# Softmax denominators in five blocks of matmul instead of seven, with one of five key additions on VectorE

## The reference

```python
scores = jnp.einsum('bhqd,bhkd->bhqk', q, k) / math.sqrt(HEAD_DIM)
causal = jnp.tril(jnp.ones((seq_len, seq_len), dtype=bool))
scores = jnp.where(causal[None, None, :, :], scores, jnp.float32(-1e+20))
attn = jax.nn.softmax(scores, axis=-1)
out = jnp.einsum('bhqk,bhkd->bhqd', attn, v)
```

## Time and profile before

| what | value |
|---|---|
| median of 3 runs | 1067.73 us (1065.66 to 1068.37) |
| the profiled execution's own time | 1066.51 us |
| its span | 1064.5 us |
| PE busy | 1017.9 us, 96% |
| PEld busy | 829.7 us, 78% |
| DVE busy | 636.3 us, 60% |
| POOL busy | 411.5 us, 39% |
| ACT busy | 399.5 us, 38% |
| mean granted TensorE clock | 0.983 |

### The profile page before, as it was taken

The page is one execution under the profiler, slowest core; times in us unless marked ns, Lnnn a source line. Parts: engine busy times, 40 slices in busy tenths (PEclk is TensorE's granted clock), DMA queues, the critical chain, the costliest instruction groups (busy, mean ns, idle before and its releaser), DMA issues.

```text
span 1064.5 us, 17672 instructions
## 1 busy us (share of the span) xinstructions
PE 1017.9 (96%) x6614; PEld 829.7 (78%) x6614; DVE 636.3 (60%) x1882; ACT 399.5 (38%) x682; POOL 411.5 (39%) x461
## 2 busy tenths in 40 slices
PE   4999999999989998999999989899999999999995
PEld 3888888898876665666666558799999999999995
DVE  7354443424447886878788636566666666666654
ACT  7132221210127775777777733222222222222221
POOL 1072552433337775777776730111122211111110
PEclk8999999999999998999999999899999999999999
DMA  9144332237237776556555344222222222222101
GB/s 354 51 158 139 119 135 103 79 124 183 96 122 193 205 197 167 144 135 159 141 137 146 114 146 137 72 89 80 79 80 79 79 81 86 82 86 86 58 20 40
DMA packets 78788, 127.31 MB, mean 120 GB/s; under 512 B 7792, under 2 KB 47088, under 8 KB 75632
## 3 DMA queue, kind: packets, MB, share of 16 engines
q1 hardware_dynamic: 78704, 126.19, 39.2%
HBM read 85.27 MB, written 40.37 MB: 118 GB/s over the span
## 4 chain that ended last, share of the span: by engine, by line
PE 88%; DVE 4%; DMA 2%; POOL 2%; ACT 2%; issue 1%; SPq 0%; POOLq 0%; DVEq 0%; ACTq 0%
PE bank L1237 19%; PE bank L1238 19%; PE bank L1239 19%; PE bank L1310 8%; PE bank L1336 7%; PE bank L1350 7%; PE bank L1367 5%; PE bank L1446 1%; DVE ln_st L928 1%; PE bank L1246 1%; DMA q_t<-shift_l 1%; DMA den_i<-inv_scratch 1%; POOL turn L656 1%; POOL turn L659 1%; DVE xt_l L945 1%
## 5 line engine op out<-in xcount | busy, mean ns | idle before, releaser
L990 DVE CUSTOM_DVE_ANT_0 bank<-bank,row_mask 128x128 f32<-128x128 f32 (+1 forms) x480 | 219.3, 523 | 62.3 <-PE bank L1310 59.0
L642 POOL TENSOR_TENSOR ln_rs<-ln_ve,minus_half 128x1 f32<-128x1 f32 x64 | 61.5, 961 | 412.2 <-DVE ln_mm L933 412.2
L815 ACT ACTIVATE prob<-bank 128x512 f32<-128x512 f32 x320 | 172.7, 599 | 38.2 <-PE bank L1336 38.0
L1237 PE MATMUL bank<-xt_h,wq_h 128*128 128x512 f32 x320 | 128.0, 400 | 4.5 <-DVE wq_l L953 4.5
L1237 PE MATMUL bank<-wf_h,xt_h 128*128 128x384 f32 (+1 forms) x384 | 129.8, 338 | 1.8 <-DVE z L1148 1.8
L1239 PE MATMUL bank<-wf_l,xt_h 128*128 128x384 f32 (+1 forms) x384 | 130.2, 339 | 0.0
L1238 PE MATMUL bank<-wf_h,xt_l 128*128 128x384 f32 (+1 forms) x384 | 130.1, 339 | 0.0
L1310 PE MATMUL bank<-k_t,q_t 96*128 96x384 f32 (+3 forms) x512 | 124.7, 340 | 2.6 <-DVE row_top L990 2.6
L1239 PE MATMUL bank<-xt_l,wq_h 128*128 128x512 f32 x320 | 125.8, 393 | 0.0
L1238 PE MATMUL bank<-xt_h,wq_l 128*128 128x512 f32 x320 | 125.8, 393 | 0.0
L1336 PE MATMUL bank<-q_t,k_t 98*128 98x512 f32 x320 | 111.4, 415 | 6.4 <-DMA q_t<-shift_l 3.1
(11 more groups left out here) (108 smaller groups left out, 1898.6 us busy)
## 6 DMA issues: line engine op xcount, KB each, us to landing
q_t<-q_scratch SPq DMA_DIRECT2D x32, 512.0 KB, 5.2
q_scratch<-turn_h SPq DMA_DIRECT2D x16, 512.0 KB, 2.7
q_scratch<-turn SPq DMA_DIRECT2D x16, 512.0 KB, 3.0
q_t<-q_scratch SPq DMA_DIRECT2D x32, 256.0 KB, 5.5
att_scratch<-att SPq DMA_DIRECT2D x32, 256.0 KB, 2.9
at_raw<-att_scratch SPq DMA_DIRECT2D x16, 512.0 KB, 3.9
x<-x SPq DMA_DIRECT2D x16, 512.0 KB, 4.3
out<-z SPq DMA_DIRECT2D x15, 512.0 KB, 2.9
```

The costliest lines, as they stand in the source:

```text
L642: nc.gpsimd.tensor_tensor(ln_rs[j][:], ln_ve[j][:], minus_half[:], ALU.pow).then_inc(count, 1)
L815: nc.scalar.activation(prob[n % 2][:, i, :, :].rearrange("p h q -> p (h q)"), bank[3 + (NS * n + i) % 3][:], ACT.Exp, scale=INV_SQRT_HD).t ...
L990: last = nc.vector.tensor_tensor_reduce(out=row, in0=row, in1=row_mask[:, SEQ - w:SEQ], scale=1.0, scalar=LOWEST, op0=ALU.add, op1=ALU.max ...
L1237: mm(dst, a_h, w_h, start=start, stop=False, skip_group_check=True)
```

## The change

Before, POOL adds three times per group: (0,2)+(1,2), (0,3)+(1,3), and (2,3) to the latter. PE streams seven column blocks of 128 per head: pairs (0,0) and (0,1) together, the two sums together, (1,1), and the diagonal pairs (2,2) and (3,3) together.

After, the two diagonal pairs are also added to the sums, once they are masked. That makes five additions: POOL does four and DVE one, (0,3)+(1,3), put between its maxima 8 and 9. PE streams five column blocks: the matmuls over (2,2) and (3,3) are gone. The addition of (2,3) on POOL now waits for DVE's (semaphore last_summed), and the two additions of diagonal pairs wait for the mask ahead of them.

```diff
+SUMS = 4
...
             def add_keys(n, i, total, a, b):
 
                 pool.wait_ge(prob_ready, NS * n + b + 1)
-                if i < 2:
+                if i == 0:
                     wait(pool, den_ps, n - 1)
+                elif i == 1:
+                    pool.wait_ge(prob_masked, TT * n + 3)
+                    pool.wait_ge(prob_summed, SUMS * n + 1)
+                elif i == 2:
+                    pool.wait_ge(last_summed, n + 1)
                 else:
-                    pool.wait_ge(prob_summed, 3 * n + 2)
+                    pool.wait_ge(prob_masked, TT * n + 4)
+                    pool.wait_ge(prob_summed, SUMS * n + 3)
...
                 add_keys(n, 0, total[:, 0, :, :], SCORES.index((0, 2)), SCORES.index((1, 2)))
-                add_keys(n, 1, total[:, 1, :, :], SCORES.index((0, 3)), SCORES.index((1, 3)))
                 mask(n, 2)
+                add_keys(n, 1, total[:, 0, :, :], None, FIRST[2])
                 add_keys(n, 2, total[:, 1, :, :], None, SCORES.index((2, 3)))
                 mask(n, 3)
+                add_keys(n, 3, total[:, 1, :, :], None, FIRST[3])
...
+            def sum_last(n):
+
+                wait(dve, den_ps, n - 1)
+                dve.wait_ge(prob_ready, NS * n + SCORES.index((1, 3)) + 1)
+                p = prob[n % 2]
+                nc.vector.tensor_tensor(key_sum[n % 2][:, 1, :, :], p[:, SCORES.index((0, 3)), :, :],
+                                        p[:, SCORES.index((1, 3)), :, :], ALU.add).then_inc(last_summed, 1)
...
-                maxima_of(6, 7, 8, 9, 10)
+                maxima_of(6, 7, 8)
+                sum_last(n)
+                maxima_of(9, 10)
...
-                pe.wait_ge(prob_summed, 3 * n + 3)
+                pe.wait_ge(prob_summed, SUMS * n + SUMS)
                 pe.wait_ge(att_ready, n + 1)
                 p, total = prob[n % 2], key_sum[n % 2]
-                for i in range(4):
-                    for h in range(REP):
-                        what, at, w = ((p[:, 0:2, h, :], 0, 2), (total[:, :, h, :], 2, 2),
-                                       (p[:, FIRST[1]:FIRST[1] + 1, h, :], 1, 1),
-                                       (p[:, FIRST[2]:FIRST[3] + 1:2, h, :], 2, 2))[i]
-                        last = mm(bank[6][HD * h:HD * h + HD, P * at:P * (at + w)].rearrange("p (b q) -> p b q", q=P),
-                                  ones[:], what, start=(i == 0), stop=(i == 3), skip_group_check=True)
+                for h in range(REP):
+                    dst = bank[6][HD * h:HD * h + HD, :].rearrange("p (b q) -> p b q", q=P)
+                    mm(dst[:, 0:2, :], ones[:], p[:, 0:2, h, :], start=True, stop=False, skip_group_check=True)
+                for h in range(REP):
...
+                    mm(dst[:, 2:4, :], ones[:], total[:, :, h, :], start=False, stop=False, skip_group_check=True)
+                for h in range(REP):
...
+                    last = mm(dst[:, 1:2, :], ones[:], p[:, FIRST[1]:FIRST[1] + 1, h, :], start=False, stop=True,
+                              skip_group_check=True)
                 last.then_inc(den_ps, 1)
```

More of the change, by code:

```diff
@@ L318, in build @@
         prob_summed = sem("prob_summed")
+        last_summed = sem("last_summed")
         den_ps = sem("den_ps")
```

## The result

The changed kernel takes 1074.61 us, median of 6 runs (1071.0 to 1076.33), against 1067.68 for the kernel before on the same occasions (6 runs). The ratio is 1.0061, with a 95% interval of 1.0042 to 1.0080. So it is slower by 0.6%, although a group has four matmuls of 256 columns less on PE. The profiled execution has a span of 1074.6 us, 10.1 above that of the kernel before. It is the slowest of the six, so the two traces lie further apart than the medians (6.9).

A forecast was written before the change was run, and what follows sets the result against it. PE was taken to set the attention stage's pace, with POOL and DVE close behind. Saving 0.43 and lateness 0.71 gave +0.28 a step, +8.1 us over 29 steps; 1067.7 + 8.1 = 1075.8, forecast 1076 us, range 1064 to 1088.

The forecast's parts named there:

- The saving: In D, PE's denominator matmuls: dropping the diagonal pairs saves 0.43 us per group, at most 13.8 us over 32 groups.
- POOL's chain: On POOL from exp 7 to the fourth mask: the longer chain alone makes V3 start 0.26 us late.
- The contention: POOL's addition of (2,2) waits for DVE's addition with two SBUF inputs, making V3 0.71 us late each step.
- Who comes first: Where both additions meet: DVE's comes at 505.74, POOL's asks at 505.82; the forecast let DVE go first, by 0.08 us.
- The rival in which POOL goes first: POOL's addition blocks DVE's: V3 0.93 us late, +0.50 to +0.70 a step, 1082 to 1088 us; chance 0.17.
- DVE's slack: DVE's addition makes its later maxima about 0.65 us late, which 0.75 us of idle time takes; cost nothing.
- The ends: Outside steps 1 to 29: the last D's saving against V3's longer wait in step 30, nothing in sum.
- the sum of +8.1: Over steps 1 to 29: -0.43 + 0.71 = +0.28 us a step, times 29 gives +8.1 us.
- The last D: At the end of the denominators, after an idle PE: the shorter matmuls should save about 0.9 us.
- PE's clock: Rival: PE's idle 0.7 us in each step lowers its clock for part of a step, above 1090 us; chance 0.03.

The follow-up runs named there:

- short D alone: The kernel before with only D's fourth set of matmuls taken out, POOL and DVE unchanged, pairs (2,2) and (3,3) missing from the denominators: 1055.8 us, ratio 0.9900.
- behind R9: The changed kernel with DVE's addition one maximum later, between the maxima of R9 and R10: 1081.1 us, ratio 1.0144.
- behind R6: The changed kernel with DVE's addition two maxima earlier, right behind the maximum of R6: 1072.8 us, ratio 1.0052.

## Why the prediction was right

**The saving.** 0.43 a step was forecast; D went from 1.65 to 1.22, and the run with the short D alone has steps of 8.97. PE did set the pace.

**POOL's chain.** V3 was to be 0.26 late from the longer chain alone. It was 0.33 (9.30 against 8.97, in two runs). Most of the difference is the semaphore between a mask and the addition that waits for it. I took 0.08 from another pair of small instructions; here it is 511.74 - 511.61 = 0.13. The 0.15 from the end of the fourth mask to V3, for which no row stood in the prediction, measured 515.41 - 515.27 = 0.14.

**The contention.** POOL's addition was to end 1.12 after DVE's. It ended at 511.74 + 1.70 = 513.44, and DVE's at 512.29, so 1.15 after. V3 was to be 0.71 late and was 0.72 late (6.30 - 5.58). The step was to be 9.68 and is 9.72; the 0.05 more of the semaphore does not count here, because DVE's end sets when POOL's addition ends. Four runs bear the cause out. Without the addition, and with its second input from PSUM, the step is 9.30, so the meeting costs 0.42 of the 9.72. With DVE's addition doubled, the two meetings cost 10.48 - 9.30 = 1.18. And with DVE second, DVE is the one that waits. The rule that the prediction named from the Trainium skill ("SBUF — State Buffer", "Who interferes with whom"), two SBUF inputs on VectorE against a GpSimd instruction that reads SBUF, agrees with all four. The 0.68 beside 1.28 with one input from PSUM is its other half.

**Who comes first.** The distance of 0.08 that I could not settle went the forecast's way, with 0.13 to spare. The rival in which POOL goes first was priced at +0.50 to +0.70 a step. The run behind R9 forces that order and gives 10.03 - 9.40 = +0.63. The price came out between its ends for another reason than the prediction gave: V3 starts 506.95 - 500.34 = 6.61 after S6, so it is 1.03 late in place of 0.93, and R4 is not stopped (the next D comes 2.20 after V3, as in the changed kernel).

**DVE's slack.** Costed at nothing, and right: DVE still idles 0.94 ahead of R2's maximum. This holds for its place alone. Two maxima earlier the same instruction costs 0.74.

**The ends.** They were set at nothing in sum, and here the sum of +8.1 hides more than it says. 28 steps x 0.32 would be 9.0. The copies of the denominators run from the first to the last like this, before and after:

```profile
L837 ACT COPY den_sb<-bank x32: 578/586/588, 327.2 to 639.8; 128x512 f32<-128x512 f32 x32
```

```profile
L846 ACT COPY den_sb<-bank x32: 577/587/587, 329.3 to 650.6; 128x512 f32<-128x512 f32 x32
```

That is 312.6 and 321.3, or +8.7. Three things stand beside the plain product.

The first is one step that the prediction did not look at, near 400 us. In it PE waits for the transfer of the shift rows, while the DMA engines are full (a share of 1.04 from 396 to 408 us before), and then it runs at half clock for some microseconds. These are busy times and clock around that step, of the kernel before, the changed kernel, and the one with the addition behind R9 (the column behind POOL is the granted clock):

```profile
408.00:412.00 4.00, 4.00 (x17) 2.34 (x21) 1.87 (x12) 1.68 (x3) 1.04 (x2) 0.50 0.58 133
```

```profile
412.00:416.00 4.00, 4.00 (x17) 2.48 (x21) 1.87 (x12) 1.68 (x3) 3.86 (x5) 0.50 0.66 150
```

```profile
412.00:416.00 4.00, 2.80 (x23) 1.60 (x27) 4.00 (x17) 1.68 (x3) 3.17 (x4) 1.00 0.91 219
```

PE idles 3.09 before and 2.69 in the changed kernel. The step is 15.98 long before and 14.62 after, so 1.36 comes back, of which the shorter wait is 0.40. Some 0.5 more is V3's wait, which this step does not have: PE is held up and POOL is not, so the fourth mask ends at 413.09 and V begins at 414.83. What the rest is was not looked for. With the addition behind R9 PE idles 1.77 there, the clock did not fall, and the step is 11.01; with the addition twice it is 10.92 (PE idles 1.68). This is the main reason why these two kernels lose less than their steps say. The length of a step does not settle the wait alone: with steps of 9.30 (without DVE's addition) PE idles 2.88, less than with 9.40, and with 9.71 (behind R6) it idles 3.27.

The second is that steps 30 and 31 are 1.8 and 0.7 us longer. In step 30 V3 asks earlier, as the prediction said, and PE idles 0.92 ahead of it. Later in that step PE waits 2.95 for an exp, where it waited 1.94. The third goes the other way. The last D saves, as forecast, 0.86:

```profile
648.21 1.08 PE L1383 MATMUL bank<-prob,ones 128*32 128x256 f32 x8 [5.00 <-ACT att L841]
...
650.50 0.80 PE L1256 MATMUL bank<-wo_h,at_h 128*128 128x512 f32 x1
```

2.29 us here and 3.15 before (636.52 to 639.67). So the three nearly cancel against the plain product: -1.7 (the 1.36, and the 0.32 that this step does not pay), +2.5 and -0.9. The prediction priced the last, named the second without a price, and did not have the first. That they came to nothing in sum is in part luck. The other 1.4 us of the span's 10.1 lie outside the denominators: the first copy comes 2.2 later and the program ends 0.7 sooner behind the last. This need not be the change. In the short D alone, which differs from the kernel before only by one shorter D up to there, the first copy comes 1.8 later too. The medians are 6.9 apart, 1.2 less than the 8.1 of the forecast. The interval of the ratio is +4.5 to +8.5 us, and it holds the 8.1.

**PE's clock.** The rival that the short gaps cost clock is out: it is 1.00 in a stretch with 5 us of them in 100.

## What to carry to other kernels

Before moving an elementwise step from GpSimd to VectorE, look at where its inputs lie. With both in SBUF it never ran beside a GpSimd instruction that reads SBUF in these traces, and its time has to be added to one of the two chains. When a list of instructions gets longer, put first what another engine waits for: here one line, the mask ahead of an addition, turned +0.6% into -0.7%. And a number that fits a theory isn't enough. The run behind R6 had the step of the wrong theory, to 0.01 us, and only its rows showed that another engine was waited for.

## What was not expected of the hardware

A blocked instruction does not start from nothing when it is released. POOL's additions, 1.28 long, ended about 1.15 after DVE's (1.70 in all in the changed kernel, 1.71 in the one with the addition twice), and DVE's, 0.68 long, ended 0.55 after POOL. And a waiting POOL instruction went ahead of a second DVE instruction that stood right behind the first (1.71 and then 1.78), while in the trace of before a mask was held by two in a row. The second of these is the one at 605.14, which starts after the mask (604.65). The first, which already ran when the mask started, is this:

```profile
603.87 1.34 DVE L1162 TENSOR_TENSOR wf_l<-wf_raw,wf_h 128x1160 fp32r<-128x1160 f32 x1
```

So the prediction's sentence that the later one waited holds for this mask only against the first of the two: the second came later than the mask and went ahead of it all the same. The mask at 617.55, which found the next wf_l running, was let in ahead of the DVE instruction behind it (1.65 in place of 1.21). What decides between these was not tried.
